# First and second attention scores multiplied in four column tiles of 32 rows, in a four-block kernel on one core

## What is computed

```python
q = jnp.einsum('bsd,hdk->bhsk', embeddings, Wq) + bq[None, :, None, :]
k = jnp.einsum('bsd,hdk->bhsk', embeddings, Wk) + bk[None, :, None, :]
v = jnp.einsum('bsd,hdk->bhsk', embeddings, Wv) + bv[None, :, None, :]
scores = jnp.einsum('bhqk,bhsk->bhqs', q, k) / jnp.sqrt(jnp.float32(dk))
scores = jnp.where(causal_mask, jnp.float32(-1000000000.0), scores)
weights = jax.nn.softmax(scores, axis=-1)
ctx = jnp.einsum('bhqs,bhsk->bhqk', weights, v)
```

## Time and profile before

| what | value |
|---|---|
| median of 3 runs | 1650.65 us (1644.73 to 1650.91) |
| the profiled execution's own time | 1646.96 us |
| its span in the trace | 1645.1 us |
| TensorE busy | 1332.7 us (81% of the span) |
| VectorE busy | 1200.2 us (73%) |
| GpSimd busy | 943.3 us (57%) |
| ScalarE busy | 916.3 us (56%) |

### The profile page before, as it was taken

The page is one execution under the profiler, slowest core; times in us unless marked ns, Lnnn a source line. Parts: engine busy times, 40 slices in busy tenths (PEclk is TensorE's granted clock), DMA queues, the critical chain, the costliest instruction groups (busy, mean ns, idle before and its releaser), DMA issues. The chain is left out here.

```text
span 1645.1 us, 25186 instructions
## 1 busy us (share of the span) xinstructions
PE 1332.7 (81%) x7232; PEld 716.4 (44%) x7235; DVE 1200.2 (73%) x2215; ACT 916.3 (56%) x1728; POOL 943.3 (57%) x779
## 2 busy tenths in 40 slices
PE   6848888888888989999926999999999998812756
PEld 2313333333333358898913244443343343212743
DVE  6999999999999554224477988889889886260325
ACT  5746666665666554456555076675666566601423
POOL 2478899988998117360756021214563654874773
PEclk9879899999999988999957599999999999955867
DMA  2019100000000025787728211211321114301317
GB/s 70 0 59 345 56 0 0 0 0 0 0 0 0 1 61 141 205 240 199 208 55 256 60 32 37 56 31 31 83 55 35 50 35 106 60 10 47 106 51 257
DMA packets 123041, 124.87 MB, mean 76 GB/s; under 512 B 31182, under 2 KB 97979, under 8 KB 120304
## 3 DMA queue, kind: packets, MB, share of 16 engines
q1 hardware_dynamic: 101032, 99.70, 21.8%
q0 software_dynamic: 10240, 15.79, 3.3%
q10 hardware_dynamic: 11656, 8.00, 1.6%
HBM read 78.52 MB, written 50.91 MB: 79 GB/s over the span
## 5 line engine op out<-in xcount | busy, mean ns | idle before, releaser
L2106 DVE TENSOR_REDUCE t_negm<-t_ps 128x1 f32<-128x512 f32 (+4 forms) x624 | 370.0, 642 | 56.7 <-PE t_ps L2374 35.2
L2083 ACT ACTIVATE t_PT<-t_ps_s 128x1024 f32<-128x1024 f32 (+3 forms) x384 | 292.1, 811 | 203.6 <-PE t_ps_s L2393 202.6
L493 POOL TENSOR_TENSOR s_HC<-s_H,X 128x1024 f32<-128x1024 f32 x128 | 307.0, 2416 | 40.3 <-DVE s_H L614 30.1
L658 PE MATMUL ps_y<-s_HC,ident 128*128 128x512 f32 x512 | 270.5, 655 | 19.8 <-POOL s_HC L493 17.9
L2011 POOL TENSOR_SCALAR_AFFINE_SELECT t_PT<-t_PT 128x512 f32<-128x512 f32 x128 | 82.7, 646 | 276.7 <-ACT t_PT L2083 276.2
L2374 PE MATMUL t_ps<-heads 96*128 96x512 bf16 (+3 forms) x640 | 201.3, 341 | 9.4 <-DVE t_negm L2106 7.6
L2393 PE MATMUL t_ps_s<-heads 96*128 96x512 bf16 (+3 forms) x768 | 181.0, 329 | 3.7 <-ACT t_PT L2083 2.1
L2408 PE MATMUL t_ps_c<-t_PT,t_VG 128*32 128x512 f32 (+3 forms) x1536 | 164.7, 502 | 1.7 <-ACT t_CT L2039 1.1
L554 ACT ACTIVATE s_dA<-m_DT,s_A 128x512 f32 (+1 forms) x192 | 127.4, 711 | 60.3 <-DVE s_H L614 59.4
L658 PEld LDWEIGHTS ps_y<-s_HC,ident 128*128 128x128 f32 x512 | 98.4, 204 | 124.1 <-issue 69.9
L1995 POOL DMA_INDIRECT slots<-X,t_idx_s x128 | 127.3, 994 | 34.9 <-issue 34.2
(11 more groups left out here) (347 smaller groups left out, 2367.2 us busy)
## 6 DMA issues: line engine op xcount, KB each, us to landing
f_w<-in_W_dram SPq DMA_DIRECT2D x93, 256.0 KB, 5.2
heads<-token_expert_rows SPq DMA_DIRECT2D x8, 1024.0 KB, 9.6
token_expert_rows<-X SPq DMA_DIRECT2D x42, 192.0 KB, 2.6
heads<-q_parts SPq DMA_DIRECT2D x42, 192.0 KB
heads<-k_parts SPq DMA_DIRECT2D x14, 576.0 KB
expert_rows<-X SPq DMA_DIRECT2D x27, 192.0 KB, 2.5
f_XS<-expert_rows SPq DMA_DIRECT2D x19, 256.0 KB
expert_rows_out<-f_YB ACTq DMA_DIRECT2D x19, 256.0 KB, 3.6
```

Of the source, the lines that this page charges most:

```text
L493: nc.gpsimd.tensor_tensor(HC[:, g % RING], H[:, g % RING], row_wide(C_sb[:, g % RING, :], 2), ALU.mult).then_inc(s_hc, 2)
L658: nc.tensor.matmul(ps_y[c][:], ident[:], HC[:, g % RING, c, :], start=g == 0, stop=g == N - 1, skip_group_check=True).then_inc(s_y, 1)
L2083: nc.scalar.activation(PT[:, n % RP, 2 * p:2 * p + 2, 0:wd], src, ACT.Exp, scale=DK ** -0.5).then_inc(s_exp, 1)
L2106: nc.vector.tensor_reduce(out, ps_1[use % BANKS1][:, 0:h * width].rearrange("p (h k) -> p h k", h=h), AX.X, ALU.max, negate=True).then_inc ...
```

## The change

Every product of the first and the second scores, which had 128 output rows, is written as four products with 32 output rows each: the stationary operand is cut into four pieces of 32 columns, each piece has its own 32 partitions of the same PSUM bank, and all four stream the same moving operand. The order of the work, the banks and the waits stay: the first of the four carries the wait, and the last of the last head's four raises the semaphore. The number of score products in the program rises from 1,920 to 7,680; the 768 products with the values are as they were.

```diff
                 for u in range(h):
                     if plain:
-                        mm = nc.tensor.matmul(out[:, u * width:u * width + plain], Q[g][0:MASK_AT, j + u, qt * P:(qt + 1) * P],
-                                              K[g][0:MASK_AT, j + u, c * CH:c * CH + plain], start=True, stop=True, skip_group_check=True)
+                        for lo in range(0, P, VW):
+                            mm = nc.tensor.matmul(out[lo:lo + VW, u * width:u * width + plain], Q[g][0:MASK_AT, j + u, qt * P + lo:qt * P + lo + VW],
+                                                  K[g][0:MASK_AT, j + u, c * CH:c * CH + plain], start=True, stop=True, skip_group_check=True)
                     if diagonal:
-                        mm = nc.tensor.matmul(out[:, u * width + plain:(u + 1) * width], Q[g][:, j + u, qt * P:(qt + 1) * P],
-                                              K[g][:, j + u, qt * P:(qt + 1) * P], start=True, stop=True, skip_group_check=True)
+                        for lo in range(0, P, VW):
+                            mm = nc.tensor.matmul(out[lo:lo + VW, u * width + plain:(u + 1) * width], Q[g][:, j + u, qt * P + lo:qt * P + lo + VW],
+                                                  K[g][:, j + u, qt * P:(qt + 1) * P], start=True, stop=True, skip_group_check=True)
                 mm.then_inc(s_p1, 1)
...
                 for h in range(2):
-                    mm = nc.tensor.matmul(ps_s[p][:, h * CH:h * CH + wd], K[g][0:MASK_AT, 2 * p + h, kt * P:(kt + 1) * P],
-                                          Q[g][0:MASK_AT, 2 * p + h, c * CH + r * P:(c + 1) * CH], start=True, stop=True)
+                    for lo in range(0, P, VW):
+                        mm = nc.tensor.matmul(ps_s[p][lo:lo + VW, h * CH:h * CH + wd], K[g][0:MASK_AT, 2 * p + h, kt * P + lo:kt * P + lo + VW],
+                                              Q[g][0:MASK_AT, 2 * p + h, c * CH + r * P:(c + 1) * CH], start=True, stop=True, skip_group_check=True)
                 mm.then_inc(s_st, 1)
```

## The result

The changed kernel takes 1638.62 us (median of 10 runs, 1634.25 to 1646.18); the kernel before took 1650.38 in 10 runs of the same comparison. The ratio, which is one of means, is **0.9942, with a 95% interval of 0.9921 to 0.9962**: 11.8 us faster by the medians and 9.6 by the ratio. That lies within the range of 1608 to 1665, but it is only about half of the 20.2 us that the sum had (1627). The sum was taken from a profiled execution 3.4 us under the median of before; from that median, 1627 is 23.4 us away.

A forecast was written before the change was run, and what follows sets the result against it. TensorE was taken to set the pace in the first sequence's head groups, VectorE next. Gains summed over the head groups to 20.2 us, taken from the profiled 1646.96 us: 1627 us, range 1608 to 1665.

The forecast's parts named there:

- Bound: In the first sequence's head groups TensorE sets the pace, 27.79 of 27.80 us; VectorE is next, 3.4 us below.
- 94% or more: Sign of being right: head groups 1 to 3 take about 26 us with VectorE busy at 94% or more.
- Step 1: Entry and exit gaps around the products with the values vanish: 12 x 0.22 = 2.6 us of TensorE a head group.
- Step 2: Full-shape operations now stand alone among tiles: about 0.2 us per contiguous block, 0.4 us a head group for two contexts.
- Step 3: Score products' four bf16 tiles stream side by side, costed at nothing; upper bound +15.3 us a head group.
- step 4: Each score product becomes four loads and four matmuls, costed at nothing; upper bound 0.029 us for each pair.
- (a): Rival: score products' weight loads come into the open, +1.4 us a head group, 1669 us; chance 0.13.
- (b): Rival: issue takes 0.029 us per tile's pair, 0.116 for a 128-column score product, 1655 us; chance 0.08.
- (d): Rival: score tiles' streams do not run side by side at this rate, 13.1 us a head group, 1857 us; chance 0.06.
- Step 5: What reaches the end: 1.8 of 2.2 us in first-sequence head groups, less where VectorE and routing fill the time; sum 20.2.
- 0.9 for the second and third: Gain of 0.9 us each in later sequences' second and third head groups, where VectorE and the routing chain fill the time.
- 1.2: Gain of 1.2 us in head group 14, which has no items but waits at the last routing.

The follow-up runs named there:

- spread loads: Changed kernel with query, key and last-layer weight loads sent in pieces, one behind each block of the next head group: 1635.07 us; kernel before edited likewise: 1650.95.
- later turn: On top of spread loads, head group 14's turned maxima put two blocks later: changed kernel 1633.43 us, kernel before 1647.62.
- Experiment 2: Query and key loads of sequences 1 to 3 left out: changed kernel 1634.46 us, kernel before 1650.57; or loads sent in pieces: 1635.07 and 1650.95.
- experiment 3: Changed kernel with only first scores in tiles of 32: 1672.5 us; only second scores: 1684.92; both scores in two tiles of 64 rows: 1659.73.
- Experiment 4: Both kernels with loads sent in pieces and head group 14's turned maxima two blocks later: changed 1633.43 us, before 1647.62.

## Why the prediction was right in direction and too large

The direction and the mechanism stood. What was forecast and found, head group by head group in us, is the kernel before less each version (in the column of the spread loads, groups 7 and 11 are taken at 29.85 and 28.40, their length in either shape where the clock did not fall; the last column is the two profiles as they are):

| head groups | forecast | tiles, spread loads | tiles as changed |
|---|---|---|---|
| 0 | 1.5 | 1.6 | 1.1 |
| 1 to 3 | 5.4 | 4.9 | 3.7 |
| 4, 8, 12 | 3.9 | 3.0 | 1.0 |
| 5, 9, 13 | 2.7 | 1.0 | 1.0 |
| 6, 10 | 1.8 | 1.9 | 1.5 |
| 7, 11 | 3.2 | 2.9 | 3.0 |
| 14 | 1.2 | -0.5 (0.6 with the later turn) | -0.8 |
| 15 | 0.5 | 0.3 | 0.4 |
| sum | 20.2 | 15.1 (16.2) | 10.8 |

Outside the groups the changed kernel's profile starts the blocks 0.7 us earlier and takes 2.2 longer behind them (217.1 against 214.9). That part took 213 to 217 us in kernels of either shape, so I read no effect of the change in it. 10.8 + 0.7 - 2.2 is the 9.3 us of the profiled executions.

- **Bound: right.** TensorE sets the pace in group 1 still: 26.05 of 26.10 us. VectorE is busy for 92% there (24.06), not for the 94% or more that was named as a sign.
- **Step 1, 2.6 us removed: right.** In group 1 the columns alone take 24.00 us in both kernels. Around and within the products with the values 2.9 us lay idle before and 0.2 after. The Trainium skill, TensorEngine Tiling, section Key Properties, says that changing the tiling mode drains TensorE; the trace agrees that such a change costs time and puts it at 0.09 to 0.15 us each way.
- **Step 2, 0.4 us added: too low.** The full shape takes 0.7 more in a group: 0.2 to 0.3 for each context, and 0.22 for the turned maxima, which had been counted at nothing. The earlier trace rows were read as "32 rows alone do not cost it"; followed through, a single tile among fours is a change of shape and had to be counted.
- **Step 3 and the loads of step 4: right.** Fours of 512 columns follow at 0.21 us, of 128 at 0.06. So (a), (b) and (d) fell. The 60 cycles for each matmul that the Trainium skill, TensorEngine Tiling, section Performance Considerations, gives do not show where four tiles run side by side: by them four would take an estimated 0.1 us.
- **Step 4, "Instructions ... I cost it at nothing": this step failed.** It looked at issue and loads alone, not at the fetch of the instructions from memory. Nearly three packets where there was one leave 5.7 us between them, and while head loads moved none came for 7.5 us. Experiment 2 shows what it costs: 3.6 to 4.1 us of the profile, where the prediction had nothing.
- **Step 5, what reaches the end: right in the groups that TensorE paces, and this step failed elsewhere.** In group 1, 0.4 us came back as longer distances among items and scores, as the 0.4 allowed for VectorE had it, and 1.6 of the 1.8 reached the end. But "0.9 for the second and third" held for the third alone. In group 5 the waits of TensorE for VectorE's banks grew, and it gained 0.3. With VectorE relieved by 8 us it gained 0.5, so VectorE's amount of work is not the cause; that the routing chain is, was argued and not tried alone. "1.2" for group 14 took its wait for one at the last routing; TensorE waited there for the last maxima (1.5 us before, 1.7 after), and the fall of the clock behind the wait was left out: with tiles 6.8 us at 1.2 GHz in all three profiles that keep the early turn and all maxima, against 3.4, none and 6.8 in three of the full shape, and none in the three mixed shapes of experiment 3. Experiment 4 shows that without the wait the group is 3.6 us shorter and the clock holds; whether tiles make the fall more frequent, or chance did in so few profiles, is open. The total came out within the range all the same, but no term had these losses in it; that the range reached so far was for the rivals' sake.

Before, in waits of TensorE in group 5 (us in total, times, longest):

```profile
PE t_ps L2374 <- DVE t_negm L2106: 1.5, 4, 0.8
```

After:

```profile
PE t_ps L2375 <- DVE t_negm L2106: 2.4, 6, 0.8
```

The forecast's closing sentence put a shortfall down to "VectorE or the routing chain". Of the 10.9 us missing in the profiled execution, 4.1 are the late fetch, 2.0 group 14, 1.7 groups 5, 9 and 13, 0.9 groups 4, 8 and 12; smaller terms and what lies outside the groups make up the rest.

## What to carry to other kernels

Products of one shape side by side, and as few changes between shapes as possible, are worth some 0.1 us for each change avoided; count every operation in TensorE's order by shape, the small transposes too. An edit that multiplies instructions also multiplies their fetch, so look at where large loads stand in the way, and send these in pieces. A wait of a microsecond or two on TensorE can cost more than itself, if the granted clock falls behind it, as it did here behind the 1.7 us of group 14.

## What was not expected of the hardware

- Instruction packets (16 KB, 256 instructions) stayed out for 7.5 us while 1.2 MB moved on another queue, and TensorE stopped for 1.0 us. The Trainium skill, Runtime: NRT & Kernel Launch, section Instruction fetch mechanics, says that crossing such a block is mostly hidden; that holds in the kernel before, where leaving the loads out changed nothing (1.0001), and not in the changed one.
- Column tiles of 64 and of 32 rows count as different shapes: with tiles of 64 beside the products, 0.10 us are lost before a product, and 0.36 - 0.21 = 0.15 from its start to the item behind it.
- With half of the maxima's work the stage ahead of the blocks fell from 45 to 29 us at a mean granted clock of 0.80 instead of 0.50. With what the head groups gained, both kernels came out 2.6% faster: far more than by the change that this document is about.
